# An attention block and a feed-forward block on one core: weight splits spread out, DMA issues shared, the residual kept in memory

## The reference, cut to what matters

```python
q = (seq2 + b_self) @ Wq + bq
k = concat([x + b_prev, seq2 + b_self]) @ Wk + bk
v = concat([x, seq2]) @ Wv + bv
score = concat([where(mask, q @ k_prev.T * SCALE, -inf), (q * k_self).sum(-1) * SCALE])
w = softmax(score)
y = x + (w[..., :-1] @ v_prev + w[..., -1:] * v_self) @ Wo + bo
h = gelu(y @ W1 + b1)
out = y + concat([h @ W2 + b2, h @ We[indices] + be[indices]], -1)
```

## Time and profile before

| | |
|---|---|
| median of three runs | 1852.75 us |
| profiled execution | 1852.25 us, its span 1850.4 us |
| TensorE | busy 1741.3 us (94%), 8320 matmuls |
| VectorE | 911.5 us (49%) |
| ScalarE | 712.2 us (38%) |
| GpSimd (POOL) | 623.7 us (34%), all of it before the rows stage |
| DMA | 132.67 MB, queue of SP 31.9% of 16 engines |

### The profile page before, as it was taken

The page is one execution under the profiler, slowest core; times in us unless marked ns, Lnnn a source line. Parts: engine busy times, 40 slices in busy tenths (PEclk is TensorE's granted clock), DMA queues, the critical chain, the costliest instruction groups (busy, mean ns, idle before and its releaser), DMA issues.

```text
span 1850.4 us, 27725 instructions
## 1 busy us (share of the span) xinstructions
PE 1741.3 (94%) x8320; PEld 1280.9 (69%) x8320; DVE 911.5 (49%) x1398; ACT 712.2 (38%) x1258; POOL 623.7 (34%) x489
## 2 busy tenths in 40 slices
PE   6999999999999999999994899999999999999997
PEld 5656656666566565665661588888888888888886
DVE  4567575775766658757576633223231323232311
ACT  3254353544544435445344432323232323333222
POOL 3177484665765748648564300000000000000000
PEclk8999999999999999999996899999999999999999
DMA  6353434424343335343335321213030302131201
GB/s 143 71 112 76 96 85 99 100 65 102 85 108 80 94 71 117 73 96 83 78 89 154 101 67 32 60 24 68 16 69 17 71 20 51 34 49 42 32 14 23
DMA packets 361052, 132.67 MB, mean 72 GB/s; under 512 B 288202, under 2 KB 328138, under 8 KB 360978
## 3 DMA queue, kind: packets, MB, share of 16 engines
q1 hardware_dynamic: 356370, 129.75, 31.9%
q10 hardware_dynamic: 4608, 2.10, 0.4%
HBM read 62.02 MB, written 18.89 MB: 44 GB/s over the span
## 4 chain that ended last, share of the span: by engine, by line
PE 72%; SPq 7%; issue 7%; POOL 5%; DMA 4%; DVE 4%; ACT 1%; POOLq 0%; DVEq 0%; ACTq 0%
PE ps_proj L1140 10%; PE ps_av L1092 6%; PE ps_av L1094 6%; PE ps_av L1093 6%; PE ps_max L1171 5%; PE ps_av L1211 5%; PE ps_proj L1092 3%; PE ps_proj L1093 3%; PE ps_proj L1094 3%; PE ps_max L1092 3%; PE ps_max L1094 3%; PE ps_max L1093 3%; PE ps_score L1094 3%; PE ps_score L1093 3%; PE ps_score L1092 3%
## 5 line engine op out<-in xcount | busy, mean ns | idle before, releaser
L647 ACT ACTIVATE p_f<-ps_score 128x512 f32<-128x512 f32 x512 | 304.4, 598 | 471.5 <-PE ps_score L1198 445.1
L839 DVE TENSOR_REDUCE m_col<-ps_max 128x1 f32<-128x512 f32 x512 | 329.1, 683 | 231.6 <-PE ps_max L1171 229.9
L542 POOL TENSOR_TENSOR p_sum<-p_sum,p_f 128x512 f32<-128x512 f32 x256 | 336.5, 1345 | 2.8 <-ACT p_f L647 2.8
L1030 DVE TENSOR_TENSOR h_lo<-h_f,h_hi 128x512 fp32r<-128x512 f32 x128 | 88.4, 691 | 478.9 <-ACT h_hi L739 478.9
L539 POOL TENSOR_TENSOR p_sum<-p_f 128x512 f32<-128x512 f32 x128 | 162.1, 1298 | 240.0 <-PE ps_av L1220 237.0
L1198 PE MATMUL ps_score<-stacks 99*128 99x512 f32 x512 | 210.1, 421 | 24.2 <-ACT p_f L647 24.1
L1171 PE MATMUL ps_max<-stacks 97*128 97x512 f32 x512 | 188.2, 435 | 41.0 <-DMA stacks<-parts 28.1
L1140 PE MATMUL ps_proj<-in_hi,w_hi 128*128 128x512 f32 x512 | 208.3, 407 | 17.7 <-POOL in_lo L547 14.3
L1140 PE MATMUL ps_proj<-in_hi,w_lo 128*128 128x512 f32 x512 | 205.7, 402 | 0.0
L1140 PE MATMUL ps_proj<-in_lo,w_hi 128*128 128x512 f32 x512 | 205.6, 402 | 0.0
L1092 PE MATMUL ps_av<-y_hi,w_hi 128*128 128x512 f32 x512 | 200.2, 391 | 5.1 <-DVE den L877 4.2
(11 more groups left out here) (126 smaller groups left out, 2644.3 us busy)
## 6 DMA issues: line engine op xcount, KB each, us to landing
stacks<-parts SPq DMA_DIRECT2D x384, 128.0 KB
raw<-in_x_dram SPq DMA_DIRECT2D x128, 64.0 KB, 2.2
raw<-in_fside_BxSxS_dram SPq DMA_DIRECT2D x128, 64.0 KB, 2.2
den<-own_scratch SPq DMA_DIRECT2D x128, 64.0 KB, 2.8
attn_scratch<-num SPq DMA_DIRECT2D x32, 256.0 KB, 3.0
a_raw<-attn_scratch SPq DMA_DIRECT2D x32, 256.0 KB, 3.6
x_raw<-in_x_dram SPq DMA_DIRECT2D x128, 64.0 KB, 2.2
we_raw<-in_L_cond_We_dram SPq DMA_DIRECT2D x32, 256.0 KB, 2.7
```

The lines of the kernel that those rows point to most:

```text
L542: pool.tensor_tensor(p_sum[:, j], p_sum[:, j], now, ALU.add).then_inc(sum_made, 1)
L647: act.activation(p_f[:, i % FLIGHT], ps_score[i % 2][:, :], ACT.Exp, scale=SCALE).then_inc(p_made, 1)
L839: dve.tensor_reduce(m_col[:, n % C, n // C:n // C + 1], ps_max[n % 2][:, :], AX.X, ALU.max).then_inc(max_made, 1)
L1030: dve.tensor_tensor(h_lo[:, m % 2], h_f[:, :], f(h_hi[:, m % 2]), ALU.subtract).then_inc(h_lo_made, 1)
```

## The change

It has four parts. The 20 pieces of Wo and W1 are taken in another order (all of a column range of W1 before the next); 12 are split in the last batch's groups 30 and 31 (`wide_at` now begins at tile (2, 0)), eight in the rows of batch 0 (`wide_late`, `wide_row`), beside W2's (`w2_row`). SP issues two of the four DMAs of `maxima`, ScalarE the other two, after the exponential of tile 11. The residual products go: VectorE sums y's parts (`whole`, rows 7 to 10), SP stores the sum in memory and fetches it, GpSimd adds it to the result before the transpose; results 2 and 3 of a batch are taken by ScalarE and VectorE after the next batch's row 0. One projection third moves from tile 5 to 6 for g = 2, and the first y's steps are moved into the attention stage or to the end of it. Parts of the diff:

```diff
 WIDE = C + C * HID // S
-WIDE_FROM = 4
-wide_at = {(2, i): (i - WIDE_FROM,) for i in range(WIDE_FROM, TILES)}
-wide_at.update({(3, i): (i + TILES - WIDE_FROM,) for i in range(WIDE - TILES + WIDE_FROM)})
+EARLY = 3 * C
+wide_at = {at: (n,) for n, at in enumerate(
+    ((2, 0), (2, 1), (2, 2), (2, 3), (2, 5), (2, 7), (2, 10), (2, 12), (2, 14), (3, 0), (3, 2), (3, 4)))}
+wide_row = {1 + n: EARLY + n for n in range(WIDE - EARLY)}
+w2_row = {0: 2, 1: 3, 2: 4, 3: 5, 9: 6, 10: 7}
+first_y_at = {(3, 10): 0, (3, 12): 1, (3, 14): 2}
 attended_at = {(3, 2 * c + 1): (c,) for c in range(C)}
...
     slots = ((4, 5, 5, 6, 7, 7, 9, 10, 11, 12, 13, 14), (0, 2, 3, 4, 5, 6, 9, 10, 11, 12, 13, 14),
-             (0, 2, 3, 5, 6, 7, 9, 10, 11, 12, 13, 15), (0, 2, 3, 4, 5, 6, 9, 10, 11, 12, 13, 15))[g]
+             (0, 2, 3, 6, 7, 7, 9, 10, 11, 12, 13, 15), (0, 2, 3, 4, 5, 6, 9, 10, 11, 12, 13, 15))[g]
     return [n for n, at in enumerate(slots) if at == i]
...
-    def maxima(b, c):
+    def maxima(b, c, tiles):
...
         sp.wait_ge(m_lo_made, G + 1)
-        for t in range(C):
+        for t in tiles:
             sp.dma_start(f(q_st[KM:KM + 2, r, :, P * t:P * (t + 1)]),
...
+    def wide_late(n):
+        sp.wait_ge(wide_lo_made, n - 3 if n < EARLY + 3 else n - 2)
+        sp.dma_start(wide_buffer(n), wide_source(n)).then_inc(late_landed[(n - EARLY) % 3], DMA)
     def attended(b, c):
         wait(sp, a_lo_made, C * b + c - 1)
+        wait(sp, sum_z_made, C * (b - 1))
         sp.dma_start(a_raw[:, c % 2], attn_dram[bass.ds(b, 1), c].rearrange("o p s -> (o p) s")).then_inc(a_landed[c % 2], DMA)
...
             if last and g == 2:
-                for n in range(10):
+                for n in range(4, 9):
                     wide(n)
             if not (last and g == C - 1):
-                maxima(*after(b, g, 1))
+                maxima(*after(b, g, 1), range(2))
             if more:
...
             if last and g == 2:
-                for n in range(10, 14):
+                for n in range(9, EARLY):
                     wide(n)
...
                 own_weights(*after(b, g, 1))
+            if last and g == 1:
+                for n in range(4):
+                    wide(n)
             if last and g == 3:
-                for n in range(14, 17):
-                    wide(n)
+                wide_late(EARLY)
                 attended(0, 2)
+                wide_late(EARLY + 1)
+                wide_late(EARLY + 2)
+                attended(0, 3)
                 residual(0, 1)
-                wide(17)
-                wide(18)
-                attended(0, 3)
-                wide(19)
                 residual(0, 2)
...
     expert_weights(0, 2)
-    for n in range(4, W2S):
+    for n in range(4, 6):
         w2_piece(n)
+        wide_late(EARLY + n - 1)
     for r in range(2):
         sp.wait_ge(attn_stored[r], DMA * C * B // 2)
+    attended(1, 0)
+    attended(1, 1)
+    w2_piece(6)
+    wide_late(WIDE - 3)
+    w2_piece(7)
     def rows(b, first, last):
-        expert_weights(b, 3)
+        if not first:
+            expert_weights(b, 3)
         if not last:
-            attended(b + 1, 0)
-            attended(b + 1, 1)
-            expert_weights(b + 1, 0)
+            if first:
+                expert_weights(b, 3)
+                wide_late(WIDE - 2)
+            else:
+                attended(b + 1, 0)
+                attended(b + 1, 1)
+                expert_weights(b + 1, 0)
             attended(b + 1, 2)
+            if first:
+                wide_late(WIDE - 1)
             attended(b + 1, 3)
+            if first:
+                expert_weights(b + 1, 0)
             residual(b + 1, 0)
             expert_weights(b + 1, 1)
+        for c in range(C):
+            keep_residual(b, c)
+        if not last:
             expert_weights(b + 1, 2)
+        for c in range(2):
+            fetch_residual(b, c)
+        if not last:
             for c in range(1, C):
...
         for c in range(C):
+            if c < 2:
+                fetch_residual(b, c + 2)
             result(b, c)
...
+    def add_residual(b, c):
+        pool.wait_ge(z_made, C * b + c + 1)
+        pool.wait_ge(fetched[c % 2], DMA * (2 * b + c // 2 + 1))
+        pool.tensor_tensor(z_f[:, c % 2], z_f[:, c % 2], a_raw[:, c % 2], ALU.add).then_inc(sum_z_made, 1)
+    def rows(b, first, last):
+        for c in range(C):
+            add_residual(b, c)
+    batches(pool, rows)
 @block.scalar
...
+    def maxima(b, c, tiles):
+        G, r = C * b + c, c % 2
+        act.wait_ge(m_lo_made, G + 1)
+        for t in tiles:
+            act.dma_start(f(q_st[KM:KM + 2, r, :, P * t:P * (t + 1)]),
+                          f(m_neg[DH * t:DH * t + 2 * HG, :])).then_inc(m_landed[r], DMA)
     def own_weight(b, c):
...
+    def whole(b, c):
+        dve.wait_ge(y_lo_made, C * b + c + 1)
+        if c >= 2:
+            dve.wait_ge(kept[c % 2], DMA * (2 * b + 1))
+        dve.tensor_tensor(a_raw[:, c % 2], f(y_hi[:, c]), f(y_lo[:, c]), ALU.add).then_inc(whole_made, 1)
     def turn_result(b, c):
-        dve.wait_ge(z_made, C * b + c + 1)
+        dve.wait_ge(sum_z_made, C * b + c + 1)
         wait(dve, stored[c % 2], (P // QUAD) * DMA * (2 * b + c // 2))
...
-    first_y_out(0)
-    first_y_out(1)
+    first_y_out(3)
+    y_low(0, 0, first_x[0])
     numerator(B - 1, C - 1)
-    y_low(0, 0, first_y[0])
-    first_y_out(2)
-    y_low(0, 1, first_y[1])
-    first_y_out(3)
-    y_low(0, 2, first_y[0])
-    y_low(0, 3, first_y[1])
+    y_low(0, 1, first_x[1])
     denominator(B - 1, C - 1)
+    y_low(0, 2, first_x[2])
+    y_low(0, 3, first_x[3])
     for n in range(4):
...
     w2_low(1)
+    dve.wait_ge(y_lo_made, C)
     expert_low(0, 0)
...
             hidden_low(b, m)
+            if m == 0 and not first:
+                for c in range(2, C):
+                    turn_result(b - 1, c)
+            if first and m in w2_row:
+                w2_low(w2_row[m])
             if first and m < 2:
-                w2_low(2 + m)
                 expert_low(b, m + 1)
-            if m == 4:
+            if m == (6 if first else 4):
                 expert_low(b, 3)
-            if first and 2 <= m < W2S - 2:
-                w2_low(2 + m)
+            if first and m in wide_row:
+                wide_low(wide_row[m])
             if not last and m in (6, 10, 14):
...
                 attended_low(b + 1, m - 3)
+            if 3 + C <= m < 3 + 2 * C:
+                whole(b, m - 3 - C)
             if not last and m == KH - 4:
...
-    def hidden(b, m, ks):
+    def hidden(b, m, ks, first):
         n = KH * b + m
+        if first and ks[0] == 0:
+            if m % C == 0:
+                pe.wait_ge(wide_lo_made, C + C * (m // C + 1))
+            if m == 0:
+                pe.wait_ge(num_made, C * B)
+            if m == 1:
+                pe.wait_ge(den_made, C * B)
         if ks[0] == 0:
...
-    def residuals(b):
-        for c in range(C):
-            wait(pe, z_made, C * (b - 1) + c + 1)
-            pe.matmul(ps_out[c][:, :], ident[:, :], y_hi[:, c], start=True, stop=False)
-            pe.matmul(ps_out[c][:, :], ident[:, :], y_lo[:, c], start=False, stop=False)
     def outputs(b, m, first):
...
                 pe.wait_ge(we_lo_made, 4 * b + m // 4 + 1)
-            mm = three(ps_out[c][:, :], left, (h_hi[:, m % 2], h_lo[:, m % 2]), False, m == KH - 1)
+            if m == 0:
+                wait(pe, z_made, C * (b - 1) + c + 1)
+            mm = three(ps_out[c][:, :], left, (h_hi[:, m % 2], h_lo[:, m % 2]), m == 0, m == KH - 1)
         mm.then_inc(out_mm, 1)
-    pe.wait_ge(wide_lo_made, WIDE)
-    pe.wait_ge(num_made, C * B)
-    pe.wait_ge(den_made, C * B)
     def rows(b, first, last):
-        for m in range(2):
-            hidden(b, m, range(C - 1))
-        for m in range(2):
-            hidden(b, m, range(C - 1, C))
-        residuals(b)
+        if first:
+            for m in range(2):
+                hidden(b, m, range(C - 1), first)
+            for m in range(2):
+                hidden(b, m, range(C - 1, C), first)
+        else:
+            for m in range(2):
+                hidden(b, m, range(C), first)
         for m in range(KH):
             if m + 2 < KH:
-                hidden(b, m + 2, range(C))
+                hidden(b, m + 2, range(C), first)
             outputs(b, m, first)
```

More of the change, by code:

```diff
@@ L202, in cond_resid_program @@
         attn_stored = [sem(f"attn_stored{r}") for r in range(2)]
+        late_landed = [sem(f"late_landed{i}") for i in range(3)]
         wide_landed = [sem(f"wide_landed{i}") for i in range(4)]
@@ L221, in cond_resid_program @@
         z_made, z_t_made = sem("z_made"), sem("z_t_made")
+        whole_made, sum_z_made = sem("whole_made"), sem("sum_z_made")
+        kept = [sem(f"kept{r}") for r in range(2)]
+        fetched = [sem(f"fetched{r}") for r in range(2)]
         stored = [sem(f"stored{r}") for r in range(2)]
@@ L399, in _ @@
                 stack(0, 1, j)
-            maxima(0, 0)
```

(25 more changed lines are left out.)

39 lines of the change are left out of this document (19 added, 20 removed).

## The result

The changed kernel took 1826.97 us (median of four runs, 1823.74 to 1832.08), the kernel before 1851.65 beside it: ratio 0.9872, 95% interval 0.9846 to 0.9899, or some 24.7 us less. On two other occasions, with nothing changed, the ratios were 0.9849 [0.9827, 0.9871] and 0.9848 [0.9823, 0.9873]. The forecast was 1818, its range 1804 to 1834: sign and range held, the gain was 6 to 9 us smaller than forecast.

The account below looks back on a forecast made before the run. TensorE's work bounds 1048 to 1838 us; before that it waits in short pieces. Attention 13, tail and first rows 11, first-row splits and loads -0.5, residual 13.1, end -2.7: 33.9 off 1852.25 gives 1818, range 1804 to 1834.

Parts of the forecast that it names:

- The maxima's issues: Attention stage: SP issuing two DMAs instead of four, with the third's move, wins 11.1 us; 13 with 2 for the clock.
- the five after them: Five groups before chunk 3, after the first two such: 0.8 us won each, 4 in all, through the third's move.
- the estimate of 0.22 us: Usual attention groups: SP's work between issues and the stack's first transfer is won, 0.22 us in 20 groups, 4.4 us.
- Rival 3: Tile 11 to 12 of every group: ScalarE's issues and SP's stack issues exclude each other; 1876 us, chance 0.06.
- The stall at tile 0: Group 30's start: ScalarE and VectorE wait for the first Wo load, 966 to 974.8; this half 6.4 us later.
- the 5 us gap before product 2: Batch 0's first rows: TensorE, without residual products, waits about 5 us and starts at the lower clock, costing 1.7 us.
- rival 1: Attention's tail gives nothing: the stall or the lower clock eats what later splits free; 1829 us, chance 0.11.
- the second half: Rest of the attention's tail: with late loads gone, tile 8's denominators end about 1015 instead of 1026.7, 11.7 us earlier.
- First rows: Batch 0's start: reordered y steps give 1.1 us, TensorE waits about 5 us; with the tail, 11 us won.
- Residual: Rows stage: 64 identity products go, 1.87 us per batch, 13.1 us over seven batches; cost at borders 0.
- rival 2: Batch borders: y's last part or h_lo 1 comes 1 to 2 us late at each of 7; 1829 us, chance 0.08.
- The chain at the end: After the last product: add, wait for chunk 3's residual, add, transpose, four issues, landing; cost 2.7 us, bounds 1.3 to 5.

Follow-up runs that it names:

- experiment 2: Kernel before with only the projection third of g = 2 moved from tile 5 to 6: 1849.29 us, ratio 0.9993.
- experiment 3: Changed kernel with all four DMAs of the maxima issued by ScalarE, none by SP: 1830.8 us, ratio 0.9881 to the kernel before.
- turn_only: Kernel before with only the weights' splits reordered and moved, and the first y's steps moved: 1844.69 us, ratio 0.9966.
- experiment 5: Changed kernel with the last batch's residual sums left in on-chip memory, no store or fetch: 1820.09 us, ratio 0.9846 to the kernel before.

## Why the prediction was right, and where it was not

**The maxima's issues: right in the sum, wrong in its terms.** The forecast took 7.1 us from the stack waits and 4 from POOL's. Stack waits fell by 14.2 us (28.1 to 13.9), POOL's by 3.2, and VectorE's maxima took 0.8 us of that back. The step of the sum that was too small is "in the five after them what comes next is a wait of 1.50 us for POOL's last input split": chunk 3's stack wait was counted as worth nothing there, since TensorE would only wait longer for POOL. But the third moved in the same diff takes that wait nearly whole when it is alone (experiment 2), so the shorter work of SP counted too. In such a group the stack wait fell from 1.5 to 0.4 us and POOL's from 1.5 to 0.7: 1.9 us together, where the forecast had 0.8. The changed kernel in such a group, where the earlier trace rows had 1.50 for POOL and the trace 1.51 for the stack:

```profile
475.68 1.36 SPq L355 DMA_DIRECT2D stacks<-m_neg  x2
476.42 1.45 ACTq L703 DMA_DIRECT2D stacks<-m_neg  x2
477.40 8.00 SPq L348 DMA_DIRECT2D stacks<-parts  x12
481.50 0.70 PE L1268 MATMUL ps_max<-stacks 97*128 97x512 f32 x2 [0.42 <-DMA stacks<-parts]
...
494.47 0.52 PE L1237 MATMUL ps_proj<-in_hi,w_hi 128*128 128x512 f32 x1 [0.68 <-POOL in_lo L601]
```

In the usual groups the estimate of 0.22 us was good: the waits went from 0.9, 0.8 and 0.53 (chunks 0, 1 and 2) to 0.67, 0.5 and 0.3. That the sum still came out near 13 is partly luck. From 60 us to group 27's end 15 us of idle time went (46.1 to 31.1), where 11.1 were forecast, and this execution's first group is 2.8 us longer, with a stretch at 1.2 GHz at 78.4 us that the execution before did not have. The trace with these two edits alone has no such stretch there and reaches group 27's end 15.8 us earlier than the kernel before (915.14 us).

**Rival 3 fell.** ScalarE's issues had a median of 0.65 us, SP's own 0.65 too, and 21 stack issues that overlapped one had a median of 0.577 us (0.597 for the rest). The trace before could have told as much: the prediction goes by one overlap, but there are 46 stack issues in it that overlap an issue of ScalarE's own weights, with a median of 0.597 like the others. The Trainium skill ("Perfetto Trace Analysis", section on the HWDGE DMA instruction) speaks of a generator locked for exclusive use; by that rule an issue that meets another's would be longer by its wait for it. The medians here don't show it; only some issues beside all four of ScalarE's do, by up to 0.3 us (experiment 3). What bounds the use of ScalarE as an issuer here is its own work: up to 930 us two issues bring no wait of TensorE for an exponential, four bring 16.2 us (experiment 3).

**The stall at tile 0: seen, but its price was too low.** Each step of it came: the load behind twelve stack issues and the own weights, the first split 4.8 us after its issue (3.9 to the landing was forecast), both engines held:

```profile
957.41 1.85 SPq L378 DMA_DIRECT2D raw<-in_L_cond_Wo_dram  x4
...
962.17 0.62 ACT L730 CAST wo_hi<-raw 128x512 fp32r<-128x512 f32 x1 [9.10 <-DMA raw<-in_L_cond_Wo_dram]
...
962.82 0.69 DVE L968 TENSOR_TENSOR wo_lo<-raw,wo_hi 128x512 fp32r<-128x512 f32 x1 [9.73 <-ACT wo_hi L730]
...
964.25 1.30 PE L1268 MATMUL ps_max<-stacks 97*128 97x512 f32 x2 [8.34 <-DVE m_col L925]
```

The forecast put this half 6.4 us later; it is 8.7 (group 27's end to group 29's, 53.1 and 61.8 us; by the forecast's own figures, 987.5 and 980.8, it should have been 6.7). What the forecast lacks there is the clock. This half in the kernel before and in the changed one, then the stall and the work behind it; TensorE's busy time is the second figure, the granted clock the third from the end:

```profile
930.97:984.10 53.13, 48.68 (x256) 28.33 (x252) 40.65 (x63) 25.00 (x48) 33.44 (x26) 0.94 0.46 123
918.36:980.13 61.77, 52.26 (x256) 29.68 (x252) 41.10 (x64) 25.58 (x49) 33.38 (x26) 0.83 0.42 110
...
955.90:964.30 8.40, 0.06 (x2) 0.07 (x1) 1.48 (x3) 2.13 (x5) 4.01 (x4) 0.69 0.71 206
964.30:980.10 15.80, 15.15 (x50) 5.90 (x54) 11.37 (x19) 5.69 (x11) 0.00 (x0) 0.52 0.28 83
```

For the same 256 products TensorE is idle 5.0 us more (4.5 and 9.5), less than forecast, and busy 3.6 us more. In the 8.3 idle us it falls to 1.2 GHz and stays there for nearly all of the 15.8 us of full work behind them. No run has the stall without its clock, so the two are told apart by these windows alone. The forecast's sum charged a lower clock to the 5 us gap before product 2, and none to the longer gap before it; only its rival 1 named it. From there the second half gained 15.8 us (42.6 to 26.9; 18.1 forecast), nearly all of it idle time (24.1 to 9.0); why it is 2.3 short is open. So denominators of group 30 end 7.1 us earlier against group 27, not 11.7; from there to product 2 it is another 1.6 shorter (28.6 against 30.2). Rival 1, that the tail gives nothing, did not come: turn_only's gain of 0.34% is the tail's.

**First rows.** TensorE's gap is 5.57 us, as written ("about 5"):

```profile
1035.55 0.79 PE L1189 MATMUL ps_av<-y_hi,w_hi 128*128 128x512 f32 x1 [5.57 <-ACT h_hi L821]
```

The stretch at 1.2 GHz that begins in it (1034.1, 6.8 us) reaches 5.4 us into the work behind it, up to 2.7 us of loss: enough for the 1.5 us that batch 0 is longer after product 2, where the kernel before had a gap of 0.67 that is gone.

**Residual: right.** All six periods from batch 1 to batch 7 are 97.92 us instead of 99.81, and the seven batches take 13.3 us less together; no period is longer than the others, so rival 2 fell. The chain at the end took the steps that were written, add, fetch of chunk 3, add, transpose, four issues:

```profile
1808.23 1.96 SPq L502 DMA_DIRECT2D out_dram<-z_t  x4
...
1810.21 1.26 POOL L636 TENSOR_TENSOR z_f<-z_f,a_raw 128x512 f32<-128x512 f32 x1 [1.53 <-DMA a_raw<-resid_scratch]
...
1813.36 1.26 POOL L636 TENSOR_TENSOR z_f<-z_f,a_raw 128x512 f32<-128x512 f32 x1 [1.89 <-DMA a_raw<-resid_scratch]
1815.47 0.71 DVE L1129 STREAM_TRANSPOSE z_t<-z_f 128x512 f32<-128x512 f32 x1 [2.80 <-DMA out_dram<-z_t]
```

Only the last releaser was not foreseen: chunk 3's transpose waits for chunk 1's store, not for the add (which ends at 1814.6). Hence the mend of experiment 5 gave 1.2 us and not 1.9.

## What to carry to other kernels

When one diff shortens two waits that follow each other, price each with the other edit in place: the forecast gave the stack wait no worth in five groups because a wait for POOL stood behind it, which the same diff shortened. (What the split of the issues gives without the third's move was not run.) A load that an in-order engine needs at a fixed place is priced from where its DMA is issued. A gap that it opens in TensorE has two prices, idle time and slower work behind it: here 5.0 and 3.6 us, after a gap of 8.3. But taking it away gave 7.5 us and not more, since other waits come to stand where it was. Issuing DMAs from a second engine is worth it while that engine has slack at that moment; beyond it the wait changes its name, and here the kernel also got slower by more than the waits tell.

## What the runs showed of the hardware

- DMA issues of ScalarE and SP overlap: with all four on ScalarE, overlapping stack issues had a median of 0.604 us against 0.598; the longest of them was 0.90.
- Executions of one kernel on one core differ by more than was thought: the kernel before from 1844.18 to 1857.68 us in 21 runs, at a mean granted clock of 0.966 to 0.975. With 10 and 13 runs the interval was still 0.18% either way (experiment 2), so three or four runs don't show a change of 0.3%.
- VectorE's subtraction of a weight's high part, with Wo loaded early, took 0.69 us at 953.21, 1.81 us at 955.02 and 1.79 us at 957.96, all three beside GpSimd's adds (six from 950.38 to 959.20): the adds alone don't make the difference, and what does was not tried. The forecast had taken 1.3.
- VectorE's multiply `num<-num,den` takes 0.69 to 1.9 us in nine of the 14 traces. In the five others one of its 32 instances takes much longer, each time beside unbroken adds of GpSimd, and ends 0.55 us after the last of them: 8.96 us (the changed kernel again), 6.47 (the residual alone) and 4.37 (the splits alone, Wo's loads earlier, the last batch in place). In the first of these it cost TensorE a wait of 6.71 us. What decides whether it gets long is open.
